# A fused gated cross-attention and feed-forward block: the down weight's lower halves all on VectorE, GpSimd's weighing of f moved ahead

## The reference

```python
x = x + tanh(g_xattn) * xattn(layernorm(x), ctx, w_xattn)       # x, ctx: 16 x 128 x 1024, float32
x = x + tanh(g_ffn) * ffn(layernorm(x), ...)

def xattn(f, e, w):   # cosine similarity of each row of e with its left neighbour, itself, its right one
    att = repeat(sim(e), C)                       # 16 x 3 x 1024, one row per shift, spread over channels
    return einsum('bit,oi->bot', unfold(f, 3) * att, w)

def ffn(h, ...):
    r = sum(top_k(h @ gate_w, 2))
    shared = relu(h @ up_w) ** 2 @ down_w         # 1024 -> 2048 -> 1024
    routed = ((h @ fc1_w) @ expert_w * r) @ fc2_w # 1024 -> 512 -> 512 -> 1024
    return layernorm(shared + routed) * ln_gamma + ln_beta
```

## Time and profile before

| what | value |
| --- | --- |
| timed runs, median (lowest to highest of 3) | 1022.1 us (1020.31 to 1025.31) |
| the profiled execution, its own time | 1020.98 us |
| its span, first to last instruction | 1019.2 us |
| mean granted PE clock | 0.98 of full speed |
| PE busy | 948.0 us |
| DVE busy | 476.0 us |
| POOL busy | 344.3 us |
| ACT busy | 322.9 us |

### The profile page before, as it was taken

One profiled execution on the slowest core, in us unless ns is written; L12 is line 12 of the kernel. 1 busy time (PEld: TensorE's weight loads), 2 busy tenths in 40 slices (PEclk: granted clock), 3 DMA queues, 4 the chain that ended last, 5 costly groups with the idle time before them and its releaser, 6 DMA issues.

```text
span 1019.2 us, 12378 instructions
## 1 busy us (share of the span) xinstructions
PE 948.0 (93%) x4562; PEld 441.1 (43%) x4562; DVE 476.0 (47%) x840; ACT 322.9 (32%) x441; POOL 344.3 (34%) x159
## 2 busy tenths in 40 slices
PE   2888799946999999999999999999999999999996
PEld 1346544412444444444444444444444444444442
DVE  6365687757355325446755125445674222221112
ACT  2557677444133212233331112233331112211111
POOL 4340225266946151133556241133654200001110
PEclk9999999977999999999999999999999999999998
DMA  8797897312241453434133363433034333200001
GB/s 347 227 313 259 302 395 262 95 45 90 73 124 42 135 206 122 129 104 113 40 117 91 98 212 128 136 103 116 24 101 134 93 105 104 83 1 1 22 21 41
DMA packets 64000, 131.29 MB, mean 129 GB/s; under 512 B 35266, under 2 KB 35394, under 8 KB 62658
## 3 DMA queue, kind: packets, MB, share of 16 engines
q1 hardware_dynamic: 63218, 127.84, 38.2%
q10 hardware_dynamic: 720, 2.62, 0.6%
HBM read 105.09 MB, written 19.07 MB: 122 GB/s over the span
## 4 chain that ended last, share of the span: by engine, by line
PE 78%; DVE 8%; ACT 3%; issue 3%; POOL 2%; DMA 2%; DVEq 2%; POOLq 1%; ACTq 0%; SPq 0%
PE psS L1337 30%; PE psR L1287 16%; PE psS L1287 16%; PE psR L1347 8%; PE psP L1255 5%; PE psP L1268 2%; DVE ring L1066 1%; POOL big L535 1%; DVE s L908 1%; DMA sim_scratch<-simo 1%; DVE s L904 1%; DMA g_col<-in_g_ffn 1%; DVEq L875 1%; POOLq L534 1%; PE psR L1393 1%
## 5 line engine op out<-in xcount | busy, mean ns | idle before, releaser
L1337 PE MATMUL psS<-big,hid 128*128 128x512 f16 x1536 | 336.8, 381 | 6.0 <-issue 5.8
L1337 PEld LDWEIGHTS psS<-big,hid 128*128 128x128 f16 x1536 | 150.2, 98 | 188.1 <-issue 8.1
L1287 PE MATMUL psS<-xT,ring 128*128 128x512 f16 (+1 forms) x912 | 191.7, 371 | 2.4 <-DVE xT L1012 1.7
L1287 PE MATMUL psR<-xT,ring 128*128 128x512 f16 (+1 forms) x912 | 190.0, 368 | 0.0
L1287 PEld LDWEIGHTS psS<-xT,ring 128*128 128x128 f16 x912 | 89.7, 99 | 102.0 <-issue 4.2
L1287 PEld LDWEIGHTS psR<-xT,ring 128*128 128x128 f16 x912 | 89.2, 98 | 97.2
L522 POOL TENSOR_TENSOR y<-y,lgb 128x1024 f32<-128x1024 f32 x15 | 39.2, 2612 | 255.5 <-ACT y L673 255.5
L1030 DVE SCALAR_TENSOR_TENSOR y<-psR,rw,y 128x1024 f32<-128x1024 f32 x15 | 19.2, 1282 | 143.6 <-PE psR L1347 143.6
L1347 PE MATMUL psR<-w,lgb 128*128 128x512 f16 x384 | 85.5, 379 | 0.0
L493 POOL TENSOR_TENSOR sides<-scr 128x1024 f32<-128x1024 f32 x12 | 29.2, 2431 | 147.1 <-DMA scr<-in_ctx 147.1
L512 POOL TENSOR_TENSOR ring<-f_buf,ring 128x1024 f32<-128x1024 f32 x18 | 39.2, 2176 | 99.0 <-ACT f_buf L641 58.9
(11 more groups left out here) (198 smaller groups left out, 998.2 us busy)
## 6 DMA issues: line engine op xcount, KB each, us to landing
ring<-pair_scratch SPq DMA_DIRECT2D x60, 512.0 KB, 3.3
ring<-sim_scratch SPq DMA_DIRECT2D x18, 504.0 KB
big<-in_w_up SPq DMA_DIRECT2D x8, 1024.0 KB, 11.1
out_rows<-y SPq DMA_DIRECT2D x15, 512.0 KB, 3.0
hid<-in_w_down SPq DMA_DIRECT2D x14, 512.0 KB, 8.0
big<-in_w_down SPq DMA_DIRECT2D x14, 512.0 KB, 6.6
scr<-in_ctx SPq DMA_DIRECT2D x12, 576.0 KB, 4.0
pair_scratch<-ring SPq DMA_DIRECT2D x12, 512.0 KB, 7.3
```

The source lines that it names most:

```text
L1287: mm = pe.matmul(up_bank[t % NR][:, cols], rows[:, a, k, :], xT[:, k, b, cols], start=(k == 0 and a == 0 and b == 0), stop=(k == KB - 1 an ...
L1337: mm = pe.matmul(psS[:, HALF * h:HALF * h + HALF], hT[:, i, a, P * j:P * j + P], dn[:, i, b, HALF * h:HALF * h + HALF], start=(i == 0 and ...
```

## The change

DVE makes LO of all sixteen row blocks of the down weight, in order. POOL makes none; `weigh(1, 0)` follows directly behind POOL's last piece of work of the up half. One semaphore, `dn_rdy`, counts the sixteen.

```diff
-        dn_rdy = [sem(f"dn_rdy{k}") for k in range(2)]
+        dn_rdy = sem("dn_rdy")
...
-        DN_POOL = [1, 4, 7, 10, 13]
-        DN_DVE = [c for c in range(IT) if c not in DN_POOL]
...
-        def dn_lo_done(c):
-            return (dn_rdy[1], DN_POOL.index(c) + 1) if c in DN_POOL else (dn_rdy[0], DN_DVE.index(c) + 1)
...
                     if first and j == 0:
-                        for k, done in enumerate((DN_DVE, DN_POOL)):
-                            sp.wait_ge(dn_rdy[k], len(done))
+                        sp.wait_ge(dn_rdy, IT)
...
-            def dn_lo(c):
-                pool.wait_ge(dn_hi, c + 1)
-                pool.tensor_scalar(dn_raw(c), dn_raw(c), wsc[:, WDN:WDN + 1], 1.0, ALU.mult, ALU.mult)
-                pool.drain()
-                pool.tensor_tensor(dn[:, c, LO, :], dn_raw(c), dn[:, c, HI, :], ALU.subtract)\
-                    .then_inc(dn_rdy[1], 1)
...
-                if first:
-                    for c in DN_POOL[0:3]:
-                        dn_lo(c)
                 weigh(m, 0)
-                if first:
-                    for c in DN_POOL[3:]:
-                        dn_lo(c)
...
                 if c >= 2:
-                    act.wait_ge(*dn_lo_done(c - 2))
+                    act.wait_ge(dn_rdy, c - 1)
...
-                    .then_inc(dn_rdy[0], 1)
+                    .then_inc(dn_rdy, 1)
...
                         for c in range(*DN_SPLIT.get(t, (0, 0))):
-                            if c in DN_DVE:
-                                dn_lo(c)
+                            dn_lo(c)
...
                         for c in DN_LATE:
-                            if c in DN_DVE:
-                                dn_lo(c)
+                            dn_lo(c)
...
                     if first:
-                        pe.wait_ge(*dn_lo_done(i))
+                        pe.wait_ge(dn_rdy, i + 1)
```

## The result

The changed kernel takes 1014.66 us (median of 6 runs, 1013.57 to 1019.0) against 1023.04 us for the kernel before in the same comparison (6 runs, 1020.31 to 1026.17). The ratio is 0.9923, with a 95% interval of 0.9902 to 0.9945: 0.8% faster, 7.9 us by the ratio. The profiled execution took 1013.57 us with a span of 1011.3, where before it was 1020.98 and 1019.2.

A forecast was written before the change was run, and what follows sets the result against it. PE was taken as the bound, standing 18.4 us for DVE's last lower half of f. The gain 12.61 - 3.4 = 9.2 us took 1020.98 to 1011.8, 1012.9 by the median; forecast 1012.5, range 1008.0 to 1017.5.

The forecast's parts named there:

- The stall and what sets it: Before xattn(1, 0), PE waits 18.4 us for DVE's last lower half of f; the down weight's splitting sets its end.
- Five lower halves at 0: One added DVE lower half per step fits the 1.30 us idle before the third: cost 0, upper bound 6.4 us.
- POOL's part gives back 12.61 us: DVE's five steps take 44.29 us, undisturbed 31.68; removing POOL's ten instructions gives back the difference, 12.61 us.
- The 2.46 of the fourth step: Share of the 12.61 us that DVE's fourth step loses, put down to POOL's weigh.
- the fifth step's 6.60: Share of the 12.61 us lost in DVE's fifth step, 4.7 of it ACT's wait for row block 10's lower half.
- The start of `weigh`: On POOL, weigh(1, 0) would start at 200.7, the middle between 199.1 and the upper bound 202.4.
- The collision: weigh's three POOL instructions beside DVE's steps two and three cost DVE 3.4 us, between bounds of 0 and 6.70.
- my two cases: At step two's third lower half, either POOL goes first, costing DVE 4.0 us, or the lower half does, costing 2.8.
- my second case: Step two's third lower half goes ahead of POOL's first weigh instruction; DVE loses 2.8 us with what the gaps absorb.
- full price of 6.70: Rival: DVE waits for each of weigh's three instructions in full; gain 5.9 us, time 1015.1 or 1016.2, chance 0.16.
- PE's own readiness and clock: Before xattn(1, 0), PE finishes row blocks 0 to 7 ten us ahead; clock stays 0.50, counted 0, bound 1.8 us gain.
- Nothing takes it back: Behind xattn(1, 0), weigh(1, 1) moves by the whole 9.2 us and xattn(1, 1) has 18.7 us of slack.

The follow-up runs named there:

- e1: The changed kernel, but DVE makes the middle lower half of each of the five steps twice, with a drain between: 1020.99 us.
- e3: The changed kernel, but weigh(1, 0) waits until row block 14 has its lower half, so POOL does nothing beside DVE's five steps: 1014.52 us.
- e4: The changed kernel with the lower halves of row blocks 1 and 4 given back to POOL, ahead of weigh(1, 0): 1017.04 us.
- e5: The changed kernel with the rest of f's work for sequence (1, 0) on ACT and DVE moved forward into the up half: 1010.9 us.
- e7: e5 plus ACT's evacuation of sequence 0 earlier, nine row blocks ahead of xattn(1, 0), POOL's beta adds spread and finish ahead of weigh(1, 2): 1004.01 us.

## Why the prediction was right, point by point

**The stall and what sets it.** Right. It was the splitting's last lower half that released PE, and the whole shift at `xattn(1, 0)` reached the end (7.92, 7.80, 7.9 us).

**Five lower halves at 0.** Right, shown by the four steps of 6.32 to 6.41 us and by e1, where one more makes the step 1.2 us longer.

**POOL's part gives back 12.61 us.** Right: e3's steps sum to 31.74 us, where the sum had 31.68, and e4 measures 1.75 for one POOL lower half where it had 1.77. Two shares inside the sum were put down wrongly, without a change to the total. The 2.46 of the fourth step are not all `weigh`: the trace of before has

```profile
210.70 3.09 POOL L535 TENSOR_TENSOR big<-big 128x1024 f16<-128x1024 f32 x1 [0.49 <-issue]
```

which had itself stood for DVE's third lower half in step three and then held up L1104 by 0.4 us in step four. And of the fifth step's 6.60, DVE waited 4.2 us longer than usual for ACT; the 4.7 is ACT's own wait.

**The start of `weigh`.** I took 200.7 between 199.1 and 202.4; it was 201.86, 6.6 us behind its last DMA issue instead of the 4.67 of the second block. Here x is loaded right behind the rows, while in the second block nothing is for 18 us; whether that is the reason was not tried.

**The collision.** This is the term that was mis-sized: 3.4 taken, 35.59 - 31.68 = 3.9 measured, where the bounds were 0 and 6.70. That the middle of my two cases came so near is partly luck. POOL's first instruction came while the lower half of row block 5 ran, which is my second case, and for that I had 2.8 where 3.9 came. The way there was wrong in one thing. I had read from two rows that DVE keeps its turn while its instructions follow without a gap. In step three the lower halves of 6 and 7 follow without a gap, and both stood, for 1.95 and 2.09 us; with 0.29 at L1085 (0.98 instead of 0.69) that is 4.3, of which the gaps took up about 0.4. All fell into one step, not into three. The rule of the Trainium skill (SBUF — State Buffer, section SBUF: two separate sides), that the one who starts holds the ports for a whole instruction and the other stands, fits these rows better than my reading. The trace of before, which I had, already holds the counter-case at 535.87 (last section). The rule's full price of 6.70 did not come, since the first of the three instructions met only the 0.29.

**PE's own readiness and clock.** PE was ready even earlier, since it started at 205.24 instead of 207.69 and did its 48 matmuls in 10.52 instead of 12.24; the granted clock was 1.00 from 205 to 208 us, behind a pause of 1.59 us, where before it was 0.50 from 205 to 210 with a pause of 5.75. So it stood 14.6 us, not the about ten that I named. This gave nothing back. The clock at 225 us is 0.50 as before, and `xattn(1, 0)` takes 5.95 us (5.83 before), so the 0 for the clock was right.

**Nothing takes it back.** Right for this change. It would not have been right for a larger one: in e5 PE begins the second sequence's row blocks 248.32 - 191.32 = 57.0 us behind the first step, held there by ACT's evacuation, and in the changed kernel 251.71 - 189.98 = 61.7. So 4.7 us more were to be had before the next stall, and the lower clock behind that stall took back 3.0 of them: `xattn(1, 1)` comes only 1.8 us earlier than in the changed kernel (266.83 - 191.32 = 75.5 behind the first step, 267.25 - 189.98 = 77.3).

**The time.** 1012.5 was forecast, 1014.66 measured. Of the 2.2 us between, 0.5 belong to the mechanism: the steps gave 8.70 us instead of 9.2. The rest is of no term: the first step started 0.77 later in the profiled execution, 2.3 us lie around its span where it was 1.8, and the median is 1.1 above the profiled execution where I had allowed 0.7. The ratio's interval puts the gain between 5.6 and 10.0 us, too wide to tell 9.2 from 8.7, so it is the traces that judge the sum.

## What to carry to other kernels

A second engine that takes a share of elementwise work can cost more than it saves: here POOL's lower half, worth 1.28 us on DVE, held DVE up by 1.8 us and, queued behind another job, ACT by 4.7. Look for the idle time that the handed-over work leaves on the first engine; if it is a gap of the same length in every step, the work fits back for nothing. And ask of each wait whether the operands were there long before: moving instructions forward in their engines' order was worth more here (1.2%, e7) than who did the work (0.8%), but only once three stalls in a row were taken away. A stall of PE can cost more than its length: the 7.9 us in e5 were followed by 72 matmuls that took 3.0 us longer at the lower clock.

## What the hardware showed unexpectedly

DVE and POOL do not take turns by one simple rule. In step three of the changed kernel two DVE instructions back to back each waited for a POOL instruction with two SBUF inputs. Before, at 252.78, the second of two back-to-back DVE instructions went ahead (1.21 us) while a POOL instruction with one SBUF input, L597, stretched to 3.14 us. The same pair of DVE instructions meets POOL again later in the trace of before, this time with two SBUF inputs on POOL:

```profile
532.68 3.27 DVE L948 TENSOR_TENSOR u_buf<-sim_side,u_buf 128x1024 f16<-128x1024 f32 x1
535.87 3.37 DVE L948 TENSOR_TENSOR u_buf<-ring,u_buf 128x1024 f16<-128x1024 f32 x1
```

```profile
535.01 3.14 POOL L524 TENSOR_TENSOR y<-y,home 128x1024 f32<-128x1024 f32 x1
```

L524 started while the first of the pair ran, and was served ahead of the second, which took 3.37 us in place of 1.21. So the kind of DVE instruction does not decide it. L597 and L524 differ in the number of SBUF inputs and also in the operation; which of the two decides was not tried.
